# PV in two runs of four units: one PSUM tile for two batches, and new instruction orders, in a graph and attention kernel

## The chip, the cores and the metric

One Trainium2 chip, one core. The metric is the device time of one execution in microseconds (us), from the profiler's first to last event of the core. The kernel before takes 847.73 us, the median of three runs (845.4 to 847.89).

## What is computed

x is (128, 128, 256) in float32: 128 independent batches of 128 nodes with 256 features. Two residual layers follow each other, and both see the same 128x128 adjacency.

```
h = relu(layernorm(x))
x = x + L0(h)      # a per-row number: max over features of (adj h) and a bias, relu
h = relu(layernorm(x))
q, k, v = h @ w_qkv                     # 8 heads of 32
attn = softmax(mask(q k^T / sqrt(32)))  # masked where adj == 0
o = (attn @ v) @ w_proj + b_proj
x = x + o + layernorm(o) * gamma + beta
```

Because L0 gives one number per row, the second layer norm of x needs no new statistics; the kernel adds that number at the end. To keep float32 accuracy with fp16 matmuls, most operands are split into a high and a low fp16 part, and three products of parts are summed.

## The kernel before

**Tiling.** The batches go in 32 groups of G = 4. A group passes through four steps of a software pipeline, so step t works on group t (layer 0, q, k and v), group t-1 (scores and their row maxima), group t-2 (transposed scores, exponentials, PV and row sums) and group t-3 (1/row sum, output projection, layer norm, store). There are 35 steps (`pipeline`, L215).

**Five programs, each with a written order.** Each engine runs the same list of items in every step; the list is the string ORDER of that engine. Each item is a letter and a number, and semaphores tie them together. A change of an ORDER string moves work in that engine's queue and nothing else.

TensorE (L278 to L477):
- K0, K1 (`mask_scores`, L333) and N0, N1 (`mask_scores_T`, L364) put the mask into the four PSUM tiles sc_ps by 16 matmuls of 32x32 tiles each. S0 to S7 (`scores`, L344) and E0 to E7 (`scores_T`, L372) add q k^T and k q^T, four matmuls each; a unit of S is a batch and half the heads. K1 waits for the exponentials of E3, N1 for the row maxima of S7.
- S0 and S4 wait until the stacks of q and k parts have landed (`stacked`). M0 (`transpose_max`, L356) transposes the row maxima; it waits until all four o tiles are read, since they share a PSUM bank.
- Q0 to Q3 (`project_qk`, L296), V0, V1 (`project_v`, L313) and L0, L1 (`layer0`, L287) share two PSUM tiles a_ps. Q0 and Q2 use the first, Q1 and Q3 the second, and V0 and V1 likewise; V0 waits for both parts of Q2, V1 for those of Q3.
- P0 to P7 (`values`, L384) multiply the exponentials of a unit (one batch, four heads) by v, in four column tiles of 32 (L400), and add the row sums in the same way (L403): 16 matmuls of 128 columns in float32 counted as two passes. P0 waits for the parts of the row maxima (`clo_ready`), since sum_ps is one bank. The PSUM tile pv_ps has room for four units, but `values` writes only its first two: P2, P4 and P6 wait until ScalarE has copied the batch before (`pv_ready`).
- R0 to R3 (`spread`, L407) spread the reciprocal row sums of a batch over the partitions, into pv_ps; O0 to O3 (`project_o`, L419) project o, into o_ps, one batch at a time.

ScalarE (L480 to L615): E0 to E7 are the exponentials (`exps`, L550), each into one of P_SLOTS = 4 buffers, so that E4 waits for P0, and so on to E7 for P3. Q0 to Q3 (`qk_high`) copy the high part of q or k; A0 to A3 (`take_pv`, L556) copy PV of a batch; C0 to C3 (`o_high`, L562), O0 to O3 (`take_o`), R and H (rectify x and its high part), M0 (`max_high`, L545), V0, V1 (`take_v`). T0 (`transpose_h`, L509) issues the DMA that transposes h from ScalarE's queue, when the low parts H0 to H3 of GpSimd are done; X0 (L528) issues the load of x three groups ahead.

VectorE (L620 to L743): S0 to S7 are the row maxima (`row_max`, L650), Q0 to Q3 the low parts of q and k (`qk_low`, L643), O0 to O3 scale o (`scale_o`, L678), I0 to I2 invert the row sums, M0 is the low part of the row maxima, L0 and L1 the maxima of layer 0, X0 and X1 the statistics of x, B and G those of o, F0 to F3 the last elementwise work (`finish`, L697), two instructions each; F0 and F1 belong to batches 0 and 1.

GpSimd (L791 to L872): C0 to C3 low parts of o (`o_low`, L818), H0 to H3 low parts of h, N0 and W0 to W3 the layer norm's factors, D0 the accumulating store of y, X0 the factors of x.

SyncE's DMA queue (L225 to L275): Q0 and Q1 (`stack_heads`, L248) each issue 12 DMAs that stack the parts of q and k by heads, when the low parts of Q1, or of Q3, are there; M0 (L241) issues two for the row maxima; C0 (`copy_x`, L235) copies x into the output, which the store adds to.

Of the kernel before, what the change touches and what calls it, by code (L numbers as in the profile page):

```python
# [56 lines left out]
def build(nc, x, adj, bias0, w_qkv, w_proj, b_proj, gamma, beta, out):  # L57
# [3 lines left out]
    with ExitStack() as ctx:  # L61
# [559 lines left out]
        def _(dve):  # L621
# [56 lines left out]
            def scale_o(g, b):  # L678
                dve.wait_ge(r_psum, G * g + b + 1)
                dve.wait_ge(pv_ready, G * g + b + 1)  # L680
                if b == 0:
                    wait(dve, ohi_ready, G * g)
# [243 lines left out]
```

## Time and profile before

| | |
|---|---|
| median of the runs | 847.73 us |
| the profiled execution | 843.2 us |
| its span, first to last instruction | 841.3 us |
| TensorE busy | 752.9 us, 89% |
| VectorE busy | 612.7 us, 73% |
| ScalarE busy | 496.4 us, 59% |
| GpSimd busy | 394.3 us, 47% |
| DMA engines, mean of 16 | 66% over three queues |
| TensorE clock granted, mean | 0.973 |

The profiled execution itself took 843.2 us, 4.5 us less than the median of the runs. Times of instructions are microseconds from the start of the span. A matmul row shows when the first of its matmuls began and how long until the last ended; ends overlap the next group's start. "PEld" are weight loads, "ACTq" and "SPq" the queues that issue DMAs. The step that is used for most rows is step 19; it begins with K0 at 471.20.

### The profile page before, as it was taken

The page shows a single profiled execution, that of the slowest core. Times are in us where ns is not written, and L with a number is a line of the kernel's source. Part 1 is how long each engine was busy: PE and PEld are TensorE (multiplying, and loading weights), DVE is VectorE, ACT ScalarE, POOL GpSimd, SP SyncE. Part 2 cuts the span into 40 slices and gives each one's busy share as a digit, 9 for nine tenths or more (in the row PEclk, how much of TensorE's full clock was granted, in tenths as well). Part 3 has the DMA queues.
Part 4 walks back from the last instruction along what each step waited for, and adds up shares of the span by engine and source line. Part 5 has one row for each costly group of instructions (what it writes and reads, how often), then busy time and mean ns, then how long its engine had stood idle before and what let it go on. Part 6 is the DMA issues. An engine that isn't in the chain of part 4 may idle for free.

```text
span 841.3 us, 28575 instructions
## 1 busy us (share of the span) xinstructions
PE 752.9 (89%) x11113; PEld 502.6 (60%) x11113; DVE 612.7 (73%) x1488; ACT 496.4 (59%) x1160; POOL 394.3 (47%) x724
## 2 busy tenths in 40 slices
PE   0668999999999999999999999999999999999662
PEld 0235666666666666666666666666666666666441
DVE  4744677777788877777788777787778887777642
ACT  3234666656666666666666666666666766655440
POOL 5712254554554444444554444554455454443442
PEclk9888999999999999999999999999999999999985
DMA  6355577778876767867767777777786887674321
GB/s 196 75 154 138 134 151 160 150 144 165 165 164 157 165 137 149 158 157 163 175 158 154 166 148 171 143 155 165 167 172 154 165 159 148 127 135 105 58 37 25
DMA packets 167285, 121.36 MB, mean 144 GB/s; under 512 B 83696, under 2 KB 166384, under 8 KB 166640
## 3 DMA queue, kind: packets, MB, share of 16 engines
q1 hardware_dynamic: 67328, 69.72, 31.2%
q10 hardware_dynamic: 82928, 33.04, 21.0%
q0 software_dynamic: 16896, 16.78, 14.3%
q8 instruction: 89, 1.46, 0.7%
q14 instruction: 44, 0.36, 0.1%
HBM read 35.06 MB, written 33.55 MB: 82 GB/s over the span
## 4 chain that ended last, share of the span: by engine, by line
PE 58%; DVE 13%; SPq 10%; issue 9%; DMA 4%; POOL 3%; ACT 3%; ACTq 1%; DVEq 0%; POOLq 0%
PE a_ps L307 13%; SPq L261 10%; DVE smax L655 9%; PE a_ps L320 7%; PE pv_ps L400 7%; PE sc_ps L380 6%; PE sum_ps L403 5%; PE sc_ps L329 5%; PE sum_ps L430 4%; PE sc_ps L352 4%; DMA stack<-pairs 3%; PE a_ps L292 2%; PE pv_ps L415 1%; POOL stack L894 1%; DVE st L688 1%
## 5 line engine op out<-in xcount | busy, mean ns | idle before, releaser
L655 DVE TENSOR_REDUCE smax<-sc_ps 128x4 f32<-128x512 f32 x256 | 164.4, 684 | 26.6 <-PE sc_ps L352 24.7
L647 DVE TENSOR_TENSOR pairs<-a_ps,pairs 128x512 f16<-128x512 f32 x128 | 87.3, 683 | 118.6 <-ACT pairs L543 118.5
L553 ACT ACTIVATE p_sb<-sc_ps 128x512 f32<-128x512 f32 x256 | 146.3, 602 | 41.0 <-PE sum_ps L403 34.3
L816 POOL TENSOR_TENSOR h_parts<-h_sb,h_parts 128x256 f16<-128x256 f32 x128 | 84.3, 670 | 137.0 <-ACT h_parts L507 136.7
L307 PE MATMUL a_ps<-hT,w_hi 128*128 128x512 f16 x512 | 135.6, 388 | 13.8 <-DMA hT<-h_parts 13.8
L822 POOL TENSOR_TENSOR oT_lo<-oT,oT_hi 128x256 f16<-128x256 f32 x128 | 85.6, 669 | 105.6 <-ACT oT_hi L566 105.3
L543 ACT ACTIVATE pairs<-a_ps 128x512 f16<-128x512 f32 x128 | 76.2, 596 | 98.1 <-issue 59.1
L400 PE MATMUL pv_ps<-p_sb,v_sb 128*32 128x128 f32 x2048 | 107.4, 278 | 16.4 <-ACT pv_sb L560 9.8
L850 POOL DMA_DIRECT2D out<-y_sb x32 | 43.1, 1348 | 162.3 <-DVE y_sb L710 162.3
L403 PE MATMUL sum_ps<-p_sb,sel_sum 128*32 128x128 f32 x2048 | 105.7, 273 | 0.0
L352 PE MATMUL sc_ps<-stack 96*128 96x128 f16 x1024 | 84.3, 222 | 11.0 <-DMA stack<-pairs 10.9
L352 PEld LDWEIGHTS sc_ps<-stack 96*128 96x128 f16 x1024 | 65.3, 99 | 34.3 <-DMA stack<-pairs 14.7
L400 PEld LDWEIGHTS pv_ps<-p_sb,v_sb 128*32 128x32 f32 x2048 | 52.3, 109 | 55.1 <-issue 47.7
L566 ACT ACTIVATE oT_hi<-oT 128x256 f16<-128x256 f32 x128 | 53.0, 414 | 48.4 <-DVE oT L684 48.3
L380 PE MATMUL sc_ps<-stack 98*128 98x128 f16 x1024 | 80.0, 222 | 0.0
L320 PE MATMUL a_ps<-w_hi,hT 128*128 128x256 f16 x512 | 77.2, 273 | 1.9 <-DVE pairs L647 1.9
L307 PEld LDWEIGHTS a_ps<-hT,w_hi 128*128 128x128 f16 x512 | 43.1, 99 | 59.7 <-issue 25.1
L307 PE MATMUL a_ps<-hT,w_lo 128*128 128x512 f16 x256 | 77.5, 385 | 0.0
L499 ACT ACTIVATE h_sb<-x_sb,shift,rstd 128x256 f32<-128x256 f32 x128 | 72.0, 588 | 7.3 <-POOL shift L809 7.3
L572 ACT ACTIVATE o_sb<-sum_ps 128x256 f32<-128x256 f32 x128 | 48.6, 380 | 44.8 <-PE sum_ps L430 42.0
L380 PEld LDWEIGHTS sc_ps<-stack 98*128 98x128 f16 x1024 | 63.8, 99 | 15.1 <-issue 13.8
L684 DVE TENSOR_TENSOR oT<-pv_ps,pv_sb 128x256 f32<-128x256 f32 x128 | 53.2, 416 | 24.0 <-PE pv_ps L415 24.0
(94 smaller groups left out, 1415.3 us busy)
## 6 DMA issues: line engine op xcount, KB each, us to landing
stack<-pairs SPq DMA_DIRECT2D x768, 64.0 KB, 3.0
out<-in_x SPq DMA_DIRECT2D x32, 512.0 KB, 4.0
out<-y_sb POOLq DMA_DIRECT2D x32, 512.0 KB, 6.6
x_sb<-in_x ACTq DMA_DIRECT2D x31, 512.0 KB, 6.0
stack<-crow SPq DMA_DIRECT2D x64, 8.0 KB, 4.1
w_sb<-in_L_gnn_w_qkv SPq DMA_DIRECT2D x1, 768.0 KB, 5.4
x_sb<-in_x SPq DMA_DIRECT2D x1, 512.0 KB, 4.3
hT<-h_parts ACTq DMA_TRANSPOSE x32, 5.9
```

What stands on the lines that cost most here:

```text
L261: nc.sync.dma_start(dst.rearrange("p s b n -> p s (b n)"), src).then_inc(stacked[j], 16)
L307: mm = nc.tensor.matmul(a_ps[c % 2][:].rearrange("p (b n) -> p b n", b=G), w[:, dc, col:col + P], hT[:, par, part, :, dc], start=(k == 0), ...
L320: mm = nc.tensor.matmul(a_ps[i][:, bb * D:(bb + 1) * D], hT[:, par, part, 2 * i + bb, dc], w[:, dc, 2 * D:3 * D], start=(k == 0), stop=(k ...
L352: mm = nc.tensor.matmul(to[:, i], stack[0:STACK, par, 0, h, b], stack[0:STACK, par, 1, h, b], start=False, stop=True, skip_group_check=True)
L380: mm = nc.tensor.matmul(to[:, i], stack[0:ROWS, par, 1, h, b], stack[0:ROWS, par, 0, h, b], start=False, stop=True, skip_group_check=True)
L400: nc.tensor.matmul(pv_ps[HD * i:HD * (i + 1), j], v_sb[:, par, b, HD * h:HD * (h + 1)], p_sb[:, u % P_SLOTS, i], start=True, stop=True)
L403: mm = nc.tensor.matmul(sum_ps[HD * i:HD * (i + 1), 0], sel_sum[:, u], p_sb[:, u % P_SLOTS, i], start=(u == 0), stop=(u == UNITS - 1), ski ...
L553: nc.scalar.activation(p_sb[:, u % P_SLOTS], sc_ps[u % SC_SLOTS][:], ACT.Exp, scale=SCALE).then_inc(p_ready, 1)
L647: nc.vector.tensor_tensor(pairs[:, 1 - c % 2, c // 2, c % 2], a_ps[c % 2][:], pairs[:, c % 2, c // 2, c % 2], ALU.subtract).then_inc(qklo_ ...
L655: nc.vector.tensor_reduce(smax[:, HC * j:HC * (j + 1), b], sc_ps[u % SC_SLOTS][:], AX.X, ALU.max).then_inc(smax_ready, 1)
L816: nc.gpsimd.tensor_tensor(h_parts[:, par, 1, b], h_sb[:, b], h_parts[:, par, 0, b], ALU.subtract).then_inc(hlo_ready, 1)
L822: nc.gpsimd.tensor_tensor(oT_lo[:, b], oT[:, b], oT_hi[:, b], ALU.subtract).then_inc(olo_ready, 1)
```

## The change

- `pv_ps` is now used in full: PV of unit u goes to slot u % 4 (PAIR = 2 * DC = 4), so the tile holds two batches. `values` waits for `pv_ready` and `v_ready` at units 0 and 4 alone.
- `take_pv`, `spread`, `scale_o` and `o_high` go by two batches: two of each in a step, each twice as wide (128x512, and four matmuls in `spread`). `o_low`, `project_o` and `take_o` stay by one batch. The semaphores count pairs accordingly.
- The ORDER strings of all five programs are new. On TensorE the eight P units stand in two runs of four, where there were four runs of two.

```
-PE   "K0 S0 S1 R0 S2 Q0 S3 R1 Q1 N0 E0 R2 O0 E1 E2 E3 L0 O1 R3 K1 S4 S5 O2 S6 S7 L1 O3 N1 M0 E4 E5 E6 "
-     "P0 P1 Q2 P2 P3 Q3 P4 P5 E7 V0 P6 P7 V1"
+PE   "K0 S0 S1 S2 R0 Q0 S3 Q1 N0 E0 R1 E1 O0 E2 E3 L0 O1 K1 S4 S5 S6 O2 L1 S7 O3 N1 E4 E5 E6 M0 E7 Q2 "
+     "P0 P1 P2 P3 Q3 V0 P4 P5 P6 P7 V1"
-ACT  "C0 Q0 R0 R1 C1 Q1 E0 C2 O0 E1 E2 E3 H0 O1 X0 C3 R2 O2 H1 H2 O3 R3 M0 H3 E4 A0 T0 Q2 A1 E5 Q3 E6 "
-     "E7 A2 V0 A3 V1 L0"
+ACT  "R0 R1 C0 Q0 H0 Q1 E0 E1 C1 O0 E2 E3 O1 X0 R2 O2 H1 R3 H2 O3 H3 M0 T0 E4 Q2 E5 L0 E6 E7 A0 Q3 V0 "
+     "A1 V1"
-DVE  "I0 I1 I2 S0 O0 S1 S2 S3 O1 Q0 O2 X0 Q1 L0 B0 O3 S4 B1 S5 S6 S7 B2 B3 M0 X1 G0 L1 Q2 F0 Q3 F1 F2 F3"
+DVE  "I0 I1 I2 S0 S1 O0 S2 S3 O1 Q0 Q1 X0 B0 S4 B1 S5 S6 S7 L0 B2 B3 M0 G0 L1 Q2 F0 F1 X1 F2 Q3 F3"
-POOL "C0 C1 C2 H0 C3 H1 H2 H3 N0 W0 W1 W2 W3 K0 D0 X0"
+POOL "C0 C1 H0 C2 C3 H1 H2 H3 N0 W0 W1 W2 W3 K0 D0 X0"
-SP   "C0 Q0 M0 Q1"
+SP   "Q0 M0 Q1 C0"
```

```diff
             def values(g, par, u, sc):
                 b, j = u // DC, u % DC
                 pe.wait_ge(p_ready, UNITS * g + u + 1)
-                if j == 0:
-                    if b % 2 == 0:
-                        pe.wait_ge(v_ready, 2 * g + b // 2 + 1)
-                    wait(pe, pv_ready, G * g + b)
+                if u % PAIR == 0:
+                    pe.wait_ge(v_ready, 2 * g + b // 2 + 1)
+                    wait(pe, pv_ready, 2 * g + b // 2)
...
-                    nc.tensor.matmul(pv_ps[HD * i:HD * (i + 1), j], v_sb[:, par, b, HD * h:HD * (h + 1)],
+                    nc.tensor.matmul(pv_ps[HD * i:HD * (i + 1), u % PAIR], v_sb[:, par, b, HD * h:HD * (h + 1)],
...
-            def spread(g, b):
+            def spread(g, i):
...
-                for j in range(DC):
-                    mm = nc.tensor.matmul(pv_ps[:, j], sel_row[:, b * DC + j].rearrange("p h d -> p (h d)"), rpair[:],
+                for n in range(PAIR):
+                    mm = nc.tensor.matmul(pv_ps[:, n], sel_row[:, PAIR * i + n].rearrange("p h d -> p (h d)"), rpair[:],
...
-            def take_pv(g, b):
-                act.wait_ge(pv_psum, UNITS * g + DC * (b + 1))
+            def take_pv(g, i):
+                act.wait_ge(pv_psum, UNITS * g + PAIR * (i + 1))
...
-                nc.scalar.activation(pv_sb[:, b], pv_ps[:, 0:DC], ACT.Copy).then_inc(pv_ready, 1)
+                nc.scalar.activation(pv_sb[:, 2 * i:2 * i + 2].rearrange("p b c n -> p (b c) n"), pv_ps[:],
+                                     ACT.Copy).then_inc(pv_ready, 1)
...
-                nc.scalar.activation(oT_hi[:, b], oT[:, b], ACT.Copy).then_inc(ohi_ready, 1)
+                nc.scalar.activation(oT_hi[:, 2 * i:2 * i + 2], oT[:, 2 * i:2 * i + 2], ACT.Copy).then_inc(ohi_ready, 1)
...
-                nc.vector.tensor_tensor(oT[:, b], pv_ps[:, 0:DC], pv_sb[:, b], ALU.mult).then_inc(oT_ready, 1)
+                nc.vector.tensor_tensor(oT[:, 2 * i:2 * i + 2].rearrange("p b c n -> p (b c) n"), pv_ps[:],
+                                        pv_sb[:, 2 * i:2 * i + 2].rearrange("p b c n -> p (b c) n"),
+                                        ALU.mult).then_inc(oT_ready, 1)
```

## Rows read from the trace of the kernel before

**Rows 1.** The page, part 4: the chain that ended last, by engine.

```profile
PE 58%; DVE 13%; SPq 10%; issue 9%; DMA 4%; POOL 3%; ACT 3%; ACTq 1%; DVEq 0%; POOLq 0%
```

**Rows 2.** Timeline of TensorE: K0 of step 4 and of step 31. Start, length, instruction.

```profile
114.89 0.43 PE L329 MATMUL sc_ps<-mask_q,identb 32*32 32x512 bf16 x16
...
752.22 0.43 PE L329 MATMUL sc_ps<-mask_q,identb 32*32 32x512 bf16 x16
```

**Rows 3.** Timeline of TensorE, step 19: K0, S0, K1's S4, N1, M0.

```profile
471.20 0.43 PE L329 MATMUL sc_ps<-mask_q,identb 32*32 32x512 bf16 x16
471.57 0.62 PE L352 MATMUL sc_ps<-stack 96*128 96x128 f16 x8
...
479.52 0.62 PE L352 MATMUL sc_ps<-stack 96*128 96x128 f16 x8
...
482.82 0.44 PE L329 MATMUL sc_ps<-mask_k,identb 32*32 32x512 bf16 x16
483.34 0.27 PE L361 MATMUL sum_ps<-identf,smax 128*32 128x128 f32 x1
483.45 0.83 PE L380 MATMUL sc_ps<-stack 98*128 98x128 f16 x12
```

**Rows 4.** Timeline of TensorE, step 19: P0, P1, Q2, P2, Q3, P4 (first rows of each).

```profile
484.47 0.42 PE L400 MATMUL pv_ps<-p_sb,v_sb 128*32 128x128 f32 x8 [0.19 <-DVE crow L661]
...
484.91 0.43 PE L400 MATMUL pv_ps<-p_sb,v_sb 128*32 128x128 f32 x8
...
485.49 1.04 PE L307 MATMUL a_ps<-hT,w_hi 128*128 128x512 f16 x4
...
486.89 0.43 PE L400 MATMUL pv_ps<-p_sb,v_sb 128*32 128x128 f32 x8
...
487.90 1.04 PE L307 MATMUL a_ps<-hT,w_hi 128*128 128x512 f16 x4
...
489.32 0.43 PE L400 MATMUL pv_ps<-p_sb,v_sb 128*32 128x128 f32 x8
```

**Rows 5.** Timeline of ScalarE, step 19: X0, M0, T0, Q2. The bracket is idle time before.

```profile
479.21 0.38 ACTq L532 DMA_DIRECT2D x_sb<-in_x  x1
...
483.64 0.27 ACT L548 ACTIVATE crow<-sum_ps 32x128 f16<-32x128 f32 x1
...
485.69 2.51 ACTq L514 DMA_TRANSPOSE hT<-h_parts  x1
...
488.31 0.60 ACT L543 ACTIVATE pairs<-a_ps 128x512 f16<-128x512 f32 x1 [2.20 <-issue]
```

**Rows 6.** Timeline of VectorE, step 19: X1, Q2, F0, Q3.

```profile
484.15 0.36 DVE L634 BATCH_NORM_AGGREGATE mv<-st 128x2 f32<-128x6 f32 x4
...
488.93 0.69 DVE L647 TENSOR_TENSOR pairs<-a_ps,pairs 128x512 f16<-128x512 f32 x1 [3.59 <-ACT pairs L543]
489.54 0.87 DVE L704 SCALAR_TENSOR_TENSOR t_sb<-o_sb,mv,w_sb 128x256 f32<-128x256 f32 x2
490.33 0.68 DVE L647 TENSOR_TENSOR pairs<-a_ps,pairs 128x512 f16<-128x512 f32 x1
```

**Rows 7.** Timeline of SyncE's DMA queue: stacks of Q3 in steps 15 and 19.

```profile
397.63 9.24 SPq L261 DMA_DIRECT2D stack<-pairs  x12
...
491.09 9.96 SPq L261 DMA_DIRECT2D stack<-pairs  x12
```

**Rows 8.** Timeline of the weight loads: S4 of step 16.

```profile
409.47 0.45 PEld L352 LDWEIGHTS sc_ps<-stack 96*128 96x128 f16 x8 [0.41 <-DMA stack<-pairs]
```

**Rows 9.** The view of line L514, T0: all 32 issues.

```profile
L514 ACTq DMA_TRANSPOSE hT<-h_parts x32: 1431/2511/3746, 15.5 to 743.5; - x32
```

**Rows 10.** The view of line L261, the stacks: from one DMA's issue to its landing.

```profile
DMA to landing us min/median/max: 2.0/3.0/6.4
```

**Rows 11.** Groups by line with their shapes: busy, mean ns of one, idle before.

```profile
L684 DVE TENSOR_TENSOR oT<-pv_ps,pv_sb 128x256 f32<-128x256 f32 x128 | 53.2, 416 | 24.0 <-PE pv_ps L415 24.0
```

**Rows 12.** The page, part 6: DMA issues with size and time to landing.

```profile
x_sb<-in_x ACTq DMA_DIRECT2D x31, 512.0 KB, 6.0
```

More of the change, by code:

```diff
@@ L50 @@
 P_SLOTS = 4
+PAIR = 2 * DC
 PAIRS = 4 * DC * G * N
@@ L387, in values @@
                 pe.wait_ge(p_ready, UNITS * g + u + 1)
-                if j == 0:
-                    if b % 2 == 0:
-                        pe.wait_ge(v_ready, 2 * g + b // 2 + 1)
-                    wait(pe, pv_ready, G * g + b)
+                if u % PAIR == 0:
+                    pe.wait_ge(v_ready, 2 * g + b // 2 + 1)
+                    wait(pe, pv_ready, 2 * g + b // 2)
                 if u == 0:
-                    wait(pe, oT_ready, G * g)
+                    wait(pe, oT_ready, 2 * g)
                     wait(pe, rsum_ready, g)
@@ L554, in exps, with o_high @@
                                      scale=SCALE).then_inc(p_ready, 1)
-            def take_pv(g, b):
-                act.wait_ge(pv_psum, UNITS * g + DC * (b + 1))
-                if b == 0:
-                    wait(act, oT_ready, G * g)
-                nc.scalar.activation(pv_sb[:, b], pv_ps[:, 0:DC], ACT.Copy).then_inc(pv_ready, 1)
-            def o_high(g, b):
-                act.wait_ge(oT_ready, G * g + b + 1)
-                if b == 0:
+            def take_pv(g, i):
+                act.wait_ge(pv_psum, UNITS * g + PAIR * (i + 1))
+                if i == 0:
+                    wait(act, oT_ready, 2 * g)
+                nc.scalar.activation(pv_sb[:, 2 * i:2 * i + 2].rearrange("p b c n -> p (b c) n"), pv_ps[:],
+                                     ACT.Copy).then_inc(pv_ready, 1)
+            def o_high(g, i):
+                act.wait_ge(oT_ready, 2 * g + i + 1)
+                if i == 0:
                     wait(act, o_psum, G * g)
-                nc.scalar.activation(oT_hi[:, b], oT[:, b], ACT.Copy).then_inc(ohi_ready, 1)
+                nc.scalar.activation(oT_hi[:, 2 * i:2 * i + 2], oT[:, 2 * i:2 * i + 2], ACT.Copy).then_inc(ohi_ready, 1)
             def take_o(g, b):
@@ L673, in invert_sums, with scale_o @@
                     dve.wait_ge(rsum16_ready, g + 1)
-                    wait(dve, r_psum, G * g)
+                    wait(dve, r_psum, 2 * g)
                     nc.vector.scalar_tensor_tensor(rpair[:], rsum16[:], lo_rows[:, 0:1], rsum[:], ALU.mult,
                                                    ALU.add).then_inc(rpair_ready, 1)
[L678 to L682, printed above, removed]
+            def scale_o(g, i):
+                dve.wait_ge(r_psum, 2 * g + i + 1)
+                dve.wait_ge(pv_ready, 2 * g + i + 1)
+                if i == 0:
+                    wait(dve, ohi_ready, 2 * g)
                     wait(dve, olo_ready, G * g)
-                nc.vector.tensor_tensor(oT[:, b], pv_ps[:, 0:DC], pv_sb[:, b], ALU.mult).then_inc(oT_ready, 1)
+                nc.vector.tensor_tensor(oT[:, 2 * i:2 * i + 2].rearrange("p b c n -> p (b c) n"), pv_ps[:],
+                                        pv_sb[:, 2 * i:2 * i + 2].rearrange("p b c n -> p (b c) n"),
+                                        ALU.mult).then_inc(oT_ready, 1)
             def stats_o(g, b):
```

27 lines of the change are left out of this document (13 added, 14 removed).

## The prediction

> **What bounds the kernel now.** I read the chain of waits first: TensorE holds 58% of it, and SyncE's DMA queue with its transfers another 14% [rows 1]. So there are two candidates, TensorE's own order and some loop that runs through SyncE. The period tells which holds when. K0 of step 4 starts at 114.89 and K0 of step 31 at 752.22 [rows 2]: 637.33 us in 27 steps, a mean of 23.60. Step 19, where TensorE hardly waits, lasts 23.20 (471.20, and K0 of step 20 at 494.40 by the same view). The mean lies 0.4 above what TensorE's order needs.
>
> The second bound is a ring that closes once per step, and the timelines of four engines give it piece by piece. S4 on TensorE at 479.52 needs the stack of q and k; from it come the row maxima, N1 at 482.82 and M0 at 483.34 [rows 3]; ScalarE reads M0 at 483.64, issues the transpose T0 at 485.69 for 2.51 us, and only then takes Q2, at 488.31: the bracket says it sat idle 2.20 us for "issue", with Q2 of TensorE long finished [rows 5]. VectorE follows with Q2 at 488.93 and Q3 at 490.33 [rows 6], SyncE starts its 12 stack DMAs at 491.09 [rows 7], and S4 of the next step waits for the last of them. From S4 to the first stack DMA it is 491.09 - 479.52 = 11.57. From the first DMA to a released S4: in step 15 it began at 397.63 [rows 7] and S4 of step 16, which did wait for it, at 409.47 [rows 8], 11.84. Between the bounds: twelve issues take 9.24 to 9.96 [rows 7]; less the last one's 0.64 and with a landing of 2.0 to 3.0 [rows 10] that is 10.6 to 12.3. I take the middle, 11.45. The ring of now is 11.57 + 11.45 = 23.02, just under the 23.20 of TensorE's order. Whenever T0 is longer than 2.51 (it reaches 3.7 [rows 9]) or the landing is late, the ring wins; that is where the 0.4 comes from.
>
> **Part 1, TensorE's order.** Nothing is added or removed among the matmuls; PV, row sums, `spread` and projections have the same counts. What goes:
> - Two of four runs of P. A run costs on both sides. Six matmuls of Q2 at 0.216 (1.04 less a length of 0.39, over three) are 1.30, but P2 comes 1.40 after Q2: 0.10 to enter. P1 to Q2 is 0.58 where P0 to P1 is 0.44 [rows 4]: 0.15 to leave. Two runs: 2 x 0.25 = 0.49.
> - P0's wait for the row maxima. E4 to E6 end 12 x 0.056 = 0.67 after 483.45 [rows 3], and 0.10 for entry gives 484.22; P0 starts at 484.47 [rows 4]. 0.25, hidden in future by E7 and Q2 (0.22 + 1.30), which stand between M0 and P0. If that cover went, 0.25 would return.
> - M0's wait for the last o tile. N1 to M0 is 0.52, K0 to S0 0.37 [rows 3]: 0.15, hidden by E4 to E6.
> - The wait of P2, P4 and P6 for the copy of one batch becomes one of P4 for two. In step 19 it is nothing (487.90 to 489.32 is 1.42, the same as 1.40) [rows 4]. In the new order Q3 and V0 stand before P4, but ScalarE has E4, Q2, E5, L0, E6, E7 before its copy. I reckon 0 to 0.2.
>
> The order then needs 23.20 - 0.49 - 0.25 - 0.15 = 22.3, to 22.5 with that wait. Alone it would be worth 23.6 - 22.5 = 1.1 us a step.
>
> The trace shows that entering and leaving column tiles costs TensorE 0.10 and 0.15 us [rows 4]. The Trainium skill (TensorEngine Tiling (Array Packing), Tiling Modes) says that a change of tiling mode drains TensorE; the trace agrees. By that rule alone the change would win some 0.5 a step, 14 us.
>
> **Part 2, VectorE, ScalarE, GpSimd.** `scale_o` takes 416 ns for 256 columns [rows 11] and, from the nearest row of 512, 0.69 [rows 6]: two for four saves 0.3 a step on an engine 73% busy, and nothing on TensorE's path: R1 now waits for a tile of 0.69 in place of 0.42, but stands behind Q0, S3, Q1, N0 and E0. The copies of 512 columns cost 0.60 [rows 5]. All that is off both paths; cost 0, between -0.3 and +0.3.
>
> **Part 3, the ring, new.** I count from S4, with durations of step 19.
> 1. S4 to N1: the same three S units, O2, L1 and O3 stand between, and the same four row maxima and one statistics instruction on VectorE: 3.30 [rows 3].
> 2. N1 to M0: 0.37 + three E units of 0.22 = 1.04, for 0.52 before. M0 at 4.34.
> 3. ScalarE's M0 at +0.30 [rows 3, 5], and T0, now directly behind it and in front of E4, some 0.27 later (M0's own length; GpSimd's low part of H3 ends about then): 4.91. T0 holds the queue 2.51, and the next starts 0.11 after [rows 5]: E4 at 7.53, Q2 behind it at 8.03 (0.60 long, the overlap of back-to-back work takes about 0.1).
> 4. VectorE's Q2 0.62 later: 8.65; the next starts 0.61 after [rows 5, 6]: 9.26. Here the new order puts F0, F1, X1 and F2 before Q3, where there was F0 alone. A pair F costs 0.79 (489.54 to 490.33), X1 about 0.30 (0.36 long) [rows 6]: 3 x 0.79 + 0.30 = 2.67. Q3 at 11.93.
> 5. SyncE starts 0.76 after (490.33 to 491.09) [rows 6, 7]: 12.69.
> 6. The landing: 11.45. C0, the copy of x, has moved from before Q0 to after Q1, the same place in the cycle, so the queue has the same two neighbours. What waits behind SyncE's stack DMAs is C0 and then Q0 of the next step, which is not late.
>
> Sum 24.14 for 23.02 before: +1.1. T0 comes earlier in the ring (4.91 for 6.17, 485.69 - 479.52), which saves 1.26; E4 behind it gives 0.50 back, and Q3 behind F1, X1 and F2 costs 1.88. The rest, 0.0, closes it: 11.57 - 1.26 + 0.50 + 1.88 = 12.69. Q2 also lets V0 go late by 0.1 to 0.2 on TensorE, which is off the ring.
>
> So the ring, not TensorE, sets the period: 24.14. There is no slack of 0.2 to swallow a long T0 any more, so every variation of T0 and of the landing passes through: I take 24.2. Against 23.60 it is +0.60 over the 28 steps in which the ring is closed, +16.8; at the end, where nothing is stacked, the shorter order gives about 0.8 back. Sum +16: the profiled execution of 843.2 becomes 859. It stands 4.5 below the median of the runs, 847.73; on the median's scale I forecast **863.5 us**, 1.9% slower.
>
> **Rivals.**
> A, TensorE is the bound (faster). If the ring came below 22.5, the period would be 22.5: 28 x -1.1 = -31, 817 us. It needs a landing of 9.8 or less. For it: twelve unhindered issues of 0.64 and 2.0 make 9.0. Against: neither row of 12 issues is near 7.7 [rows 7]. Chance 0.12.
> B, the ring binds but is shorter by 0.5 to 1.2, since T0 issues in 2.0 or stacks land in 10.6, both inside their rows [rows 9, 10]: period 23.0 to 23.7, 831 to 850 us. It decides against me from a ring of 23.6, so 0.54 off my sum. Chance 0.20, of which 0.08 lies within 0.3% of no change (about what a measurement of this kernel can tell from none).
> C, the landing gets longer (slower still). X0, the load of x, is issued at 479.21, 0.31 before S4 [rows 5, 3]. It hangs on O1, not on S4; with S4 late it starts about 1.4 before S4, beside the last stacks, and needs 6.0 to land [rows 12]. If the last 1.4 ran at half rate, +0.7 and 36 us in all: 874 to 884 us. Chance 0.16.
> The Trainium skill (DMA: Bandwidth & Descriptors, Queues, rings and completion order) says that each DMA engine goes round the queue rows by packets, so a second queue takes its share; no row here isolates it, and its case is C's.
> D, the change does not do what it says: P4 waits for its copy as long as P2, P4 and P6 did. Worth 0.2 a step, 6 us, inside my forecast's range.
>
> **How the numbers follow.** Forecast (ring 23.8 to 24.6, 852 to 874 us) 0.52; A 0.12; B 0.20; C 0.16. Faster 0.12 + 0.12 = 0.24, same 0.08, slower 0.52 + 0.16 = 0.68. The range 836 to 880 leaves out A and part of B (0.13) and the top of C (0.06). The forecast's own range is 852 to 874.
>
> **What the new profile would show.** P runs of four units with one entry and exit each; M0 and P0 without idle time before them; K1 to S4 with about 1.4 us of idle time, released by the stack DMAs, in nearly every step; "issue" before E4 rather than before Q2 on ScalarE; SyncE's second dozen starting 12.7 after S4. I am wrong if S4 waits in few steps, if the dozen starts under 12.1 after S4, or if its landing is under 11. A gain with S4 not waiting would be A.

## The result, and the profile after the change

| | before | after |
|---|---|---|
| median of 5 runs | 847.73 us (845.4 to 848.78) | 868.32 us (866.44 to 869.51) |
| ratio, with its 95% interval | | 1.0259 (1.0224 to 1.0294) |
| profiled execution: time, span | 843.2, 841.3 us | 866.44, 864.5 us |
| mean period, K0 of step 4 to K0 of step 31 | 23.60 us | 24.33 us |

The changed kernel is 2.6% slower. The forecast was 863.5 us, and the measured median lies 4.8 us above it. Two of the ten executions of the kernel with X0 late (below) were slow, one with 965.59 us at a granted clock of 0.748, and its ratio leaves both out though its median counts them.

**What bounds it.** The first part of the page of the changed kernel gives the engines' busy time; the chain that ended last, by engine, is its fourth part.

```profile
PE 749.8 (87%) x11113; PEld 504.0 (58%) x11113; DVE 603.9 (70%) x1424; ACT 469.1 (54%) x1032; POOL 395.2 (46%) x724
...
SPq 29%; DVE 22%; PE 19%; DMA 8%; issue 7%; ACTq 6%; ACT 4%; POOL 3%; DVEq 0%; POOLq 0%
```

TensorE held 58% of the chain before [rows 1] and holds 19% now; SyncE's queue with its transfers went from 14% to 37%, VectorE from 13% to 22%, ScalarE's queue from 1% to 6%. That is the ring: S4, row maxima, N1, M0, T0, Q2, the pairs F, Q3, twelve stack DMAs ("the dozen"), their landing, S4. No engine does more work: VectorE and ScalarE have 64 and 128 instructions fewer than before and less busy time in all.

The waits of TensorE between 100 and 740 us, changed kernel: line, releaser, us in total, times, longest.

```profile
PE sc_ps L353 <- DMA stack<-pairs: 16.0, 21, 2.5
PE a_ps L321 <- DVE pairs L648: 14.0, 20, 1.1
PE sum_ps L427 <- ACT o_sb L573: 5.0, 22, 0.3
```

And the same view of the kernel before:

```profile
PE pv_ps L400 <- DVE crow L661: 5.5, 27, 0.3
PE pv_ps L400 <- ACT pv_sb L560: 5.2, 10, 0.8
PE sc_ps L352 <- DMA stack<-pairs: 3.0, 5, 1.2
```

P's two small waits are gone, as the change was made to do, 10.7 us in all. In their place stand S4's for the stack, V0's for Q2 (L321) and O1's for its accumulator (L427), 35.0 us.

**One turn of the ring, step 12.** TensorE's timeline of the changed kernel, from S4 of step 12 (the scores right behind K1) to K0 of step 13, with S4 of step 13 as the last row:

```profile
325.18 0.84 PE L353 MATMUL sc_ps<-stack 96*128 96x128 f16 x12 [0.27 <-DMA stack<-pairs]
...
328.49 0.44 PE L330 MATMUL sc_ps<-mask_k,identb 32*32 32x512 bf16 x16
...
329.54 0.27 PE L362 MATMUL sum_ps<-identf,smax 128*32 128x128 f32 x1
...
331.27 0.43 PE L400 MATMUL pv_ps<-p_sb,v_sb 128*32 128x128 f32 x8
...
333.15 1.04 PE L308 MATMUL a_ps<-hT,w_hi 128*128 128x512 f16 x4
...
335.17 0.60 PE L321 MATMUL a_ps<-w_hi,hT 128*128 128x256 f16 x4 [0.55 <-DVE pairs L648]
...
336.58 0.43 PE L400 MATMUL pv_ps<-p_sb,v_sb 128*32 128x128 f32 x8
...
339.88 0.43 PE L330 MATMUL sc_ps<-mask_q,identb 32*32 32x512 bf16 x16
...
349.81 0.45 PE L353 MATMUL sc_ps<-stack 96*128 96x128 f16 x5 [0.92 <-DMA stack<-pairs]
```

ScalarE's: M0, T0, E4, Q2.

```profile
329.85 0.27 ACT L548 ACTIVATE crow<-sum_ps 32x128 f16<-32x128 f32 x1 [0.69 <-PE sum_ps L362]
330.01 3.11 ACTq L514 DMA_TRANSPOSE hT<-h_parts  x1
333.22 0.60 ACT L553 ACTIVATE p_sb<-sc_ps 128x512 f32<-128x512 f32 x1 [3.10 <-PE sum_ps L403]
333.71 0.59 ACT L543 ACTIVATE pairs<-a_ps 128x512 f16<-128x512 f32 x1
```

VectorE's: Q2, then F0 and F1 (two L707, two L713), X1 (L635), F2, and only then Q3.

```profile
334.34 0.69 DVE L648 TENSOR_TENSOR pairs<-a_ps,pairs 128x512 f16<-128x512 f32 x1 [3.05 <-ACT pairs L543]
334.94 0.87 DVE L707 SCALAR_TENSOR_TENSOR t_sb<-o_sb,mv,w_sb 128x256 f32<-128x256 f32 x2
335.73 0.87 DVE L713 SCALAR_TENSOR_TENSOR y_sb<-t_sb,base,beta_sb 128x256 f32<-128x256 f32 x2
336.52 0.37 DVE L635 BATCH_NORM_AGGREGATE mv<-st 128x2 f32<-128x6 f32 x4
336.82 0.84 DVE L707 SCALAR_TENSOR_TENSOR t_sb<-o_sb,mv,w_sb 128x256 f32<-128x256 f32 x2
337.58 0.68 DVE L648 TENSOR_TENSOR pairs<-a_ps,pairs 128x512 f16<-128x512 f32 x1
```

SyncE's queue, the dozen of Q3:

```profile
338.34 9.98 SPq L262 DMA_DIRECT2D stack<-pairs  x12
```

The four lists read as one chain: 325.18 to N1 at 328.49 is 3.31, to M0 1.05, to T0 0.47, T0 itself 3.11 and 0.10 to E4, 0.49 to Q2, 0.63 to VectorE's Q2, 3.24 to Q3, 0.76 to the first stack DMA, together 13.16; from there to the next S4 11.47. One turn is 24.63 us. ScalarE's bracket before E4 blames a PE line that had ended long before: P's row sums of the step before. What stood in front of E4 was T0, issued from the same queue and 3.11 long; a bracket whose releaser had long finished does not name what held the instruction.

TensorE's list shows what the change gained: one run of P from 331.27 and one from 336.58, each entered and left once, and neither M0 nor P0 has a bracket. It also shows V0 at 335.17, 2.02 after Q3 began, where six matmuls and their hand-over would take 1.30.

**Over steps 6 to 27**, worked out from the trace in this way. The rows that do not say median are means.

| us | forecast | after |
|---|---|---|
| S4 to N1; to M0; to T0, medians | 3.30; 4.34; 4.91 | 3.30; 4.35; 4.83 |
| the same, means | | 3.44; 4.49; 4.97 |
| T0, median of all issues | 2.51 | 3.02 (mean 2.86) |
| VectorE, Q2 to Q3 | 3.28 | 3.30 (median 3.24) |
| S4 to the first DMA of the dozen | 12.69 | 13.17 (12.19 to 13.87) |
| first DMA to the last landing | 11.45 | 11.12 (10.55 to 12.97) |
| landing to S4 | 0, always | 0.05, in every step |
| period | 24.2 | 24.33 |

In the kernel before, the same means are 11.74 to the dozen, 11.39 for the landing and then 0.51 in which the stack lay ready and TensorE came late. Now 13.17 + 11.12 + 0.05 = 24.34: S4 waits for the landing in every step, so the ring is the period.

**TensorE's clock.** Medians and means of the first row differ because of two steps, 7 and 21. In them S4 had waited 2.5 and 2.4 us for the stack, with TensorE idle, and the granted clock then stood at 0.50 (1.2 in place of 2.4 GHz) for 3.4 us. Here is the view of windows for step 7 (the granted clock is the third value from the right), with S4 and N1 of that step:

```profile
197.80:204.50 6.70, 4.27 (x69) 2.80 (x53) 3.52 (x8) 4.99 (x12) 3.23 (x5) 1.00 0.76 190
204.60:207.90 3.30, 3.15 (x20) 2.47 (x21) 2.21 (x4) 0.15 (x1) 0.00 (x0) 0.50 0.91 259
```

```profile
204.75 1.46 PE L353 MATMUL sc_ps<-stack 96*128 96x128 f16 x12 [2.46 <-DMA stack<-pairs]
...
209.56 0.44 PE L330 MATMUL sc_ps<-mask_k,identb 32*32 32x512 bf16 x16
```

The twelve matmuls of S4 take 1.46 where they take 0.84 in step 12, and N1 starts 4.81 after S4 in place of 3.30 (4.74 in step 21). The kernel before has the clock at 1.00 all the way from step 4 to step 31. In the twelve traces of this document there are 324 steps between K0 of step 4 and K0 of step 31. Of these, 19 hold a stretch at 0.50, and they last 25.95 us or more; none of the other 305 lasts over 25.73. In all 19, S4 had waited 1.8 to 4.7 us for the stack just before. A late ring thus costs more than its own wait. That the wait brings the clock down was not tested by itself, and not every wait does (`before_x_early`, step 12: 2.19 us, and the clock stays at 1.00).

### The profile page after: what moved, and what is told of

The parts are those of the page before. It is cut to its first block, busy times and chain, and to the rows that moved or that the text cites. A ratio compares the mean times of both kernels' runs of the same rounds, so it can differ in the third digit from the quotient of the medians.

```text
span 864.5 us, 28255 instructions
## 1 busy us (share of the span) xinstructions
PE 749.8 (87%) x11113; PEld 504.0 (58%) x11113; DVE 603.9 (70%) x1424; ACT 469.1 (54%) x1032; POOL 395.2 (46%) x724
## 3 DMA queue, kind: packets, MB, share of 16 engines
q0 software_dynamic: 16896, 16.78, 14.5%
q8 instruction: 89, 1.46, 0.7%
## 4 chain that ended last, share of the span: by engine, by line
SPq 29%; DVE 22%; PE 19%; DMA 8%; issue 7%; ACTq 6%; ACT 4%; POOL 3%; DVEq 0%; POOLq 0%
SPq L262 29%; DVE smax L656 8%; DMA stack<-pairs 8%; DVE t_sb L707 6%; ACTq L514 6%; PE a_ps L308 4%; PE sc_ps L381 4%; DVE y_sb L713 2%; PE sc_ps L353 2%; DVE pairs L648 2%; ACT pairs L543 2%; PE sc_ps L330 2%; PE pv_ps L400 2%; PE sum_ps L430 2%; PE sum_ps L403 1%
## 5 line engine op out<-in xcount | busy, mean ns | idle before, releaser
L553 ACT ACTIVATE p_sb<-sc_ps 128x512 f32<-128x512 f32 x256 | 142.7, 606 | 92.1 <-PE sum_ps L403 90.4
L648 DVE TENSOR_TENSOR pairs<-a_ps,pairs 128x512 f16<-128x512 f32 x128 | 85.1, 683 | 97.6 <-ACT pairs L543 97.5
L824 POOL TENSOR_TENSOR oT_lo<-oT,oT_hi 128x256 f16<-128x256 f32 x128 | 83.1, 670 | 89.9 <-ACT oT_hi L567 89.8
L400 PE MATMUL pv_ps<-p_sb,v_sb 128*32 128x128 f32 x2048 | 105.1, 276 | 3.7 <-ACT pv_sb L560 3.0
L353 PE MATMUL sc_ps<-stack 96*128 96x128 f16 x1024 | 81.4, 224 | 26.7 <-DMA stack<-pairs 26.2
L403 PE MATMUL sum_ps<-p_sb,sel_sum 128*32 128x128 f32 x2048 | 103.6, 273 | 0.0
L321 PE MATMUL a_ps<-w_hi,hT 128*128 128x256 f16 x512 | 77.1, 273 | 15.6 <-DVE pairs L648 15.6
L381 PE MATMUL sc_ps<-stack 98*128 98x128 f16 x1024 | 83.4, 222 | 0.0
L381 PEld LDWEIGHTS sc_ps<-stack 98*128 98x128 f16 x1024 | 65.0, 99 | 16.2 <-issue 14.9
L685 DVE TENSOR_TENSOR oT<-pv_ps,pv_sb 128x512 f32<-128x512 f32 x64 | 43.9, 686 | 40.4 <-PE pv_ps L415 40.4
L400 PEld LDWEIGHTS pv_ps<-p_sb,v_sb 128*32 128x32 f32 x2048 | 56.9, 109 | 23.8 <-issue 20.2
L321 PEld LDWEIGHTS a_ps<-w_hi,hT 128*128 128x128 f16 x512 | 45.9, 97 | 39.0 <-ACT pairs L543 23.8
```

Source lines behind the costliest of these rows:

```text
L321: mm = nc.tensor.matmul(a_ps[i][:, bb * D:(bb + 1) * D], hT[:, par, part, 2 * i + bb, dc], w[:, dc, 2 * D:3 * D], start=(k == 0), stop=(k ...
L353: mm = nc.tensor.matmul(to[:, i], stack[0:STACK, par, 0, h, b], stack[0:STACK, par, 1, h, b], start=False, stop=True, skip_group_check=True)
L381: mm = nc.tensor.matmul(to[:, i], stack[0:ROWS, par, 1, h, b], stack[0:ROWS, par, 0, h, b], start=False, stop=True, skip_group_check=True)
L400: nc.tensor.matmul(pv_ps[HD * i:HD * (i + 1), u % PAIR], v_sb[:, par, b, HD * h:HD * (h + 1)], p_sb[:, u % P_SLOTS, i], start=True, stop=True)
L403: mm = nc.tensor.matmul(sum_ps[HD * i:HD * (i + 1), 0], sel_sum[:, u], p_sb[:, u % P_SLOTS, i], start=(u == 0), stop=(u == UNITS - 1), ski ...
L553: nc.scalar.activation(p_sb[:, u % P_SLOTS], sc_ps[u % SC_SLOTS][:], ACT.Exp, scale=SCALE).then_inc(p_ready, 1)
```

## The experiments

All kernels were timed against the kernel before on the same chip; a ratio is the kernel's time over that of the kernel before (843.05 to 846.39 us there). My theory is the ring; its rival is that the wider tiles or TensorE's new order cost the time by themselves. None of the expectations has a term for TensorE's clock.

### Landing shortened, in both kernels

The store of y, which adds into `out` from GpSimd's queue, is cut to 16 of its 128 rows; nothing on an engine's path changes.

```diff
-                nc.gpsimd.dma_start(og[g], y_sb[:], accum_op=ALU.add).then_inc(stored, 16)
+                nc.gpsimd.dma_start(og[g][0:16], y_sb[0:16], accum_op=ALU.add).then_inc(stored, 16)
```

> The changed kernel, but the store of y covers only 16 of the 128 rows of each batch; the rest of the output lacks the last addition. The question is whether the ring (S4, M0, T0, Q2, Q3, the dozen stack DMAs, their landing, S4) sets the period. Ring theory: the store shares the DMA engines with the dozen, so without most of it the dozen lands in about 10.0 us in place of 11.1 (mean, from its first issue), and the whole 1.1 a step comes off: 868 - 30 = about 838 us. Rival, the loss lies on TensorE's side (the wider copies, V0 and P4 waiting) and the stacks only seem late: the landing gets shorter and the period stays within 0.3 of 24.3, 860 us or more.

> The kernel before with the same store of 16 rows in 128; the rest of the output lacks the last addition. Ring theory: here TensorE's own order needs 23.2 of the 23.6 us of a step, so however early the dozen lands, no more than about 0.3 a step comes off: 838 to 843 us, a gain of 5 to 10 us against some 30 in the changed kernel with the same edit. Rival (the store slows every kernel alike, through memory or the engines): both kernels gain the same.

Changed kernel: 836.51 us, ratio 0.9889 (0.9826 to 0.9952), against 1.0259 with the whole store. Kernel before: 835.5 us, ratio 0.9895 (0.986 to 0.9931). The same edit is worth 3.6% in one and 1.05% in the other. The landing fell by 1.3 us in both (11.12 to 9.84, 11.39 to 10.14), the period from 24.33 to 23.38 and from 23.60 to 23.38. TensorE's waits in the changed kernel with the small store, 100 to 740 us:

```profile
PE a_ps L321 <- DVE pairs L648: 17.2, 22, 1.3
PE sc_ps L353 <- DMA stack<-pairs: 1.3, 4, 0.4
```

S4's 16.0 us are 1.3, and the clock stays at 1.00 from step 4 to step 31. V0's wait stays, so it belongs to another loop. That a transfer which no engine waits for makes the difference between the two kernels speaks for the ring and against a cost of tiles or matmuls.

### One segment of the ring lengthened in the kernel before

Q3 on VectorE put behind F1 and F2, as the change has it; nothing else.

```diff
-  "... M0 X1 G0 L1 Q2 F0 Q3 F1 F2 F3"
+  "... M0 X1 G0 L1 Q2 F0 F1 F2 Q3 F3"
```

> The kernel before with one move in VectorE's order: Q3 behind F1 and F2, as the change has it (tiles, TensorE, ScalarE as before). Ring theory: first stack DMA 1.6 us later after S4 (13.3 for 11.7), ring 13.3 + 11.4 = 24.7, +1.1 a step, some 30 us: about 875. Rival, Q3's place costs nothing since SyncE waits for something else or V1 hides it: under 852.

890.1 us, ratio 1.0567 (1.05 to 1.0635): this one move of the change, alone, costs twice what the whole change costs. From S4 to the dozen it is 13.40 instead of 11.74 on the mean, and TensorE's first wait between 100 and 740 us is now:

```profile
PE sc_ps L352 <- DMA stack<-pairs: 35.6, 21, 4.7
```

It is 15 us slower than I expected, and four steps lasted 29.1 to 30.6 us. Each has two things in it. The first is a landing of 14.5 to 14.9 just before, on which S4 waits over 4 us. The second is the clock: it then stands at 0.50 for 3.4 us, once for 6.8, and S4 to N1 takes 4.8 and once 6.1 in place of 3.3. With a fifth such step, of 26.7 us, the clock costs 8.9 us between S4 and N1 alone. The long landings bring the mean landing to 11.87, 12.7 us in 27 steps. The two together are more than what I missed by; in the steps at full clock S4 to the dozen is 13.10, under my 13.3.

X0, the load of x, began some 5 us before S4 in the four, but that is because S4 came late: it starts 9.8 to 10.0 after the dozen's first DMA there, and 9.7 to 10.9 after it in the steps that land in 10.4 to 12.6 too. What goes with the four long landings is a slow issue, 10.8 to 11.2 for the dozen where it is 9.0 to 10.5 in the others. In the kernel before, where X0 stands 11.4 after the first DMA, two dozens of 10.9 landed in 12.4; so a slow issue that reaches into the load of x may be what makes them 14.5 and more. No run here separates the two.

### The load of x beside the stacks (rival C)

In the kernel before, X0 moves to the head of ScalarE's order.

```diff
-  "C0 Q0 R0 R1 C1 Q1 E0 C2 O0 E1 E2 E3 H0 O1 X0 C3 ..."
+  "X0 C0 Q0 R0 R1 C1 Q1 E0 C2 O0 E1 E2 E3 H0 O1 C3 ..."
```

> The kernel before with only X0 moved, to the head of ScalarE's order. The load of x then starts about 3.4 us after the dozen. Contention theory: the dozen takes 13.1 us for 11.4, the ring 11.7 + 13.1 + 0.05 = 24.9 closes over TensorE's 23.2, and the time rises by 1.2 a step, some 33 us, to about 877. Rival, two transfers side by side just share idle bandwidth (the DMA engines are 76% busy): landing within 0.4 of before, under 855 us.

876.56 us, ratio 1.0407 (1.0378 to 1.0435), as expected. SyncE's queue, then ScalarE's, then the weight load of the S4 that follows:

```profile
335.66 9.36 SPq L261 DMA_DIRECT2D stack<-pairs  x12
...
339.49 0.38 ACTq L532 DMA_DIRECT2D x_sb<-in_x  x1
...
348.69 0.45 PEld L352 LDWEIGHTS sc_ps<-stack 96*128 96x128 f16 x8 [1.36 <-DMA stack<-pairs]
```

The dozen is issued in the usual time, 9.36 us, yet S4 starts 13.03 after its first DMA. On the mean the landing went from 11.39 to 13.36: 512 KB whose transfer lies wholly beside the dozen add 2.0 us, and the load itself takes 8.0 us by its median where it took 6.0 [rows 12]. The Trainium skill (DMA: Bandwidth & Descriptors, Queues, rings and completion order) says that a DMA engine goes round the queue rows packet by packet; that both transfers are longer together agrees with it. In the changed kernel X0 stands 0.90 before S4 on the mean, and 10.3 after the dozen's first DMA in nearly every step. Its landing is 11.12 all the same, so rival C added nothing to the mean. The two landings of 12.90 and 12.97 stand before the two steps at half clock; why they are long is open. In the kernel with X0 at the head the clock falls to 0.50 in four of the 27 steps, each time behind a wait of S4.

### Parts of the ring shortened in the changed kernel

Q2 directly behind T0 on ScalarE, for E4 first:

```diff
-  "... M0 T0 E4 Q2 E5 L0 E6 E7 A0 Q3 V0 A1 V1"
+  "... M0 T0 Q2 E4 E5 L0 E6 E7 A0 Q3 V0 A1 V1"
```

> The changed kernel with one swap in ScalarE's order: Q2 directly behind T0, E4 behind Q2. It takes one exponential, 0.48 us, out of the ring and touches nothing else. Ring theory: 0.4 a step less, 868 - 11 = about 857 us, and first stack DMA of Q3 about 12.7 after S4 in place of 13.2. Rival, VectorE is late for Q3 anyway since it works off F0 to F2: no gain, since F0 starts when Q2 is done, this rival could only hold if VectorE were busy before Q2, where the trace shows it idle. Second rival: E4 to E7 get late and P4 waits for its copy, 0.3 or more a step, no gain.

A miss: 871.63 us, ratio 1.0327 (1.0284 to 1.0369), not the 857 I expected. From S4 to the dozen it fell to 12.92 only, and the landing rose by 0.6 to 11.76. TensorE's waits:

```profile
PE sc_ps L353 <- DMA stack<-pairs: 26.4, 22, 4.1
PE pv_ps L400 <- ACT pv_sb L560: 6.7, 16, 0.6
PE a_ps L321 <- DVE pairs L648: 6.3, 12, 1.1
```

V0's wait halved, P4 waits for its copy (rival D), and the longest S4 wait is 4.1 for 2.5. The clock falls three times, once for 6.8 us, where it fell twice before. With the steps touched by that left out, S4 to the dozen is 12.70 for 13.09 in the changed kernel, so the swap did give the 0.4 that I expected of it; but the landing is 11.61 for 11.08 in the same steps, which takes it back. Why the landing grew is not settled by this run.

Q3 early on both engines of its way:

```diff
 ScalarE
-  "... M0 T0 E4 Q2 E5 L0 E6 E7 A0 Q3 V0 A1 V1"
+  "... M0 T0 E4 Q2 E5 Q3 L0 E6 E7 A0 V0 A1 V1"
 VectorE
-  "... L1 Q2 F0 F1 X1 F2 Q3 F3"
+  "... L1 Q2 F0 Q3 F1 X1 F2 F3"
```

> The changed kernel with Q3 alone moved: on ScalarE behind E5, on VectorE behind F0 (so F1, X1 and F2 come after it). It undoes the part of the change that I price highest. Ring theory: the first stack DMA comes at most 11.4 after S4 in place of 13.2, the stacks no longer hold S4 in most steps, and the period falls to the next bound, T0 in front of Q2 and so of V0, about 23.8: 868 - 14 = about 854 us. Rival, T0's issue alone is to blame: no gain over 3 us.

855.25 us, ratio 1.0125 (1.0054 to 1.0196), as expected, against 1.0259. The dozen starts 11.28 after S4 instead of 13.17. TensorE's waits:

```profile
PE pv_ps L400 <- ACT pv_sb L560: 18.3, 27, 1.1
PE a_ps L321 <- DVE pairs L648: 11.6, 18, 1.0
PE sc_ps L353 <- DMA stack<-pairs: 1.4, 2, 0.8
```

The ring is open and S4 no longer waits, but the gain is 13 us, not the 1.89 a step that the ring gave: ScalarE now reaches the copy A0 later, so P4 waits 0.7 a step, and V0 still waits for Q2 behind T0. Three conditions hang on one engine's order, and undoing one brings up the next.

### New orders on three engines, X0 first and X0 late

TensorE's order stays that of the change; ScalarE, VectorE and GpSimd get new ones. The two kernels differ only in X0's place.

```diff
 ScalarE
-  "R0 R1 C0 Q0 H0 Q1 E0 E1 C1 O0 E2 E3 O1 X0 R2 O2 H1 R3 H2 O3 H3 M0 T0 E4 Q2 E5 L0 E6 E7 A0 Q3 V0 A1 V1"
+  "X0 R0 H0 C0 Q0 R1 H1 Q1 E0 E1 O0 E2 E3 C1 O1 R2 H2 O2 R3 H3 O3 M0 T0 Q2 E4 E5 Q3 A0 E6 E7 A1 V0 L0 V1"
   (second kernel: X0 between O2 and R3)
 VectorE
-  "I0 I1 I2 S0 S1 O0 S2 S3 O1 Q0 Q1 X0 B0 S4 B1 S5 S6 S7 L0 B2 B3 M0 G0 L1 Q2 F0 F1 X1 F2 Q3 F3"
+  "I0 I1 I2 S0 O0 S1 S2 S3 Q0 X0 Q1 X1 O1 L0 B0 S4 S5 S6 S7 B1 B2 B3 G0 M0 L1 F0 Q2 F1 Q3 F2 F3"
 GpSimd
-  "C0 C1 H0 C2 C3 H1 H2 H3 N0 W0 W1 W2 W3 K0 D0 X0"
+  "C0 H0 C1 H1 C2 C3 H2 H3 N0 K0 W0 W1 X0 W2 W3 D0"
```

> The changed kernel with TensorE's order, tiles and wide copies untouched, and new orders for ScalarE, VectorE and GpSimd: statistics B2, B3 and G0 before M0, F0 before Q2 and only F1 between Q2 and Q3 on VectorE; on ScalarE Q2 directly behind T0 and Q3 before E6; H1 to H3 earlier. By the durations of the trace the ring falls from 24.3 to 22.5 and TensorE's order, 22.4 to 22.6, becomes the bound. Ring theory: period 22.6, 868 - 1.7 x 28 = about 821 us, below the 848 of the kernel before; the gain of the runs of four shows once the ring is out of the way. Rival, the tile for two batches costs on TensorE or ScalarE by itself: not under 848.

> The run after_three_orders was 854 us where 821 had been expected: its ring up to the first stack DMA did fall to 11.1 us, but the dozen took about 12.9 us to land in place of 11.1, and there ScalarE's order had put the load of x (X0) at the head of the step, 3.4 us after the dozen's start. This kernel is the same but for X0, which stands behind O2, so after S4, when no dozen is in flight. Contention theory: the landing returns to 11.1 to 11.4, the period falls from 24.0 to 22.6 to 22.9, about 854 - 34 = 820 us. Rival, the shorter ring makes the landing long in some other way (SyncE's queue fuller, the store): the landing stays over 12.4 and the time over 840.

With X0 first: 854.48 us, ratio 1.0117 (1.0068 to 1.0166). With X0 late: 836.01 us, ratio 0.9894 (0.9858 to 0.993). Both missed my 821 and 820, and by different things. X0 first, SyncE's dozen, the load of x and the next S4:

```profile
328.48 9.30 SPq L262 DMA_DIRECT2D stack<-pairs  x12
...
331.79 0.38 ACTq L532 DMA_DIRECT2D x_sb<-in_x  x1
...
341.21 0.45 PEld L353 LDWEIGHTS sc_ps<-stack 96*128 96x128 f16 x8 [1.50 <-DMA stack<-pairs]
```

X0 late, the same three:

```profile
324.00 9.49 SPq L262 DMA_DIRECT2D stack<-pairs  x12
...
335.62 0.67 PEld L353 LDWEIGHTS sc_ps<-stack 96*128 96x128 f16 x12 [0.23 <-issue]
...
337.34 0.38 ACTq L532 DMA_DIRECT2D x_sb<-in_x  x1
```

In the first, x comes 3.3 after the dozen's first DMA and S4 starts 12.73 after it; in the second, x comes after S4 and S4 starts 11.62 after. The mean landings are 12.9 and 11.70, the periods 24.03 and 23.31. From S4 to the dozen it is 11.1 and 11.3, some 1.9 less than in the changed kernel; X0's place alone is worth the other 2.2%, with what the clock adds: it fell three times in the first and once in the second. The second stays 1.0 above the 22.3 that TensorE's order needs. That goes with a ring of 11.32 + 11.70 = 23.0 and a wait of V0 of 0.46 a step.

### New orders on four engines, with the changed tiles and with those of before

First the changed tiles:

```diff
 TensorE
-  "... R0 Q0 S3 Q1 N0 E0 R1 E1 O0 E2 E3 L0 O1 K1 S4 S5 S6 O2 L1 S7 O3 N1 E4 E5 E6 M0 E7 Q2 P0 P1 P2 P3 Q3 V0 ..."
+  "... R0 Q0 S3 Q1 N0 E0 R1 E1 O0 E2 E3 L0 O1 K1 S4 S5 O2 S6 S7 L1 O3 N1 E4 M0 E5 E6 Q2 E7 Q3 P0 P1 P2 P3 V0 ..."
 ScalarE
+  "R0 Q0 H0 C0 Q1 E0 E1 C1 O0 E2 E3 R1 O1 R2 H1 X0 O2 H2 R3 H3 O3 M0 T0 Q2 Q3 E4 E5 A0 L0 E6 E7 A1 V0 V1"
 VectorE
+  "I0 I1 I2 S0 S1 O0 S2 S3 Q0 O1 Q1 B0 B1 S4 S5 S6 S7 B2 L0 B3 G0 M0 L1 X0 X1 Q2 Q3 F0 F1 F2 F3"
 GpSimd
+  "H0 C0 C1 C2 C3 H1 H2 H3 N0 K0 W0 W1 W2 W3 X0 D0"
```

> The changed tiles with new orders for TensorE, ScalarE, VectorE and GpSimd: M0 behind E4, Q2 and Q3 before P0, Q2 and Q3 directly behind T0 on ScalarE and behind each other on VectorE, X0 between H1 and O2. By the durations of the traces the ring is 9.6 + 11.2 = 20.8 and TensorE's order needs 22.2: period 22.2 to 22.5, about 868 - 1.9 x 28 = 814 us, well below the kernel before. If the landing grows over 12.5, or T0 makes Q0 of the next step late, it would be 22.8 or more, over 825 us.

808.16 us, ratio 0.9588 (0.9557 to 0.9619). It beats the kernel before by 4.1% and the changed one by 6.5% (0.9588 / 1.0259). Its chain:

```profile
PE 74%; SPq 6%; ACTq 5%; DVE 4%; POOL 3%; DMA 3%; issue 2%; ACT 2%; DVEq 0%; POOLq 0%
```

All waits of TensorE that the view lists between 100 and 700 us:

```profile
PE a_ps L321 <- DVE pairs L648: 3.4, 7, 0.8
PE sc_ps L353 <- DMA stack<-pairs: 0.9, 3, 0.4
```

K0 of step 4 and of step 31:

```profile
111.88 0.43 PE L330 MATMUL sc_ps<-mask_q,identb 32*32 32x512 bf16 x16
...
716.95 0.43 PE L330 MATMUL sc_ps<-mask_q,identb 32*32 32x512 bf16 x16
```

605.07 / 27 = 22.41, and eleven of the 27 steps last 22.20 to 22.21, which is what the order of matmuls needs. From S4 to the dozen it is 9.74: M0 stands behind one E unit instead of three, and Q2 and Q3 go through ScalarE and VectorE before anything that can wait. With a landing of 11.79 the ring takes 21.53, and 0.84 of slack stands before S4. This is rival A, at an order of 22.2 where I had 22.3 to 22.5.

Then new orders of the same aim for the kernel before, its tiles and its copies by one batch kept:

```diff
 TensorE
-  "K0 S0 S1 R0 S2 Q0 S3 R1 Q1 N0 E0 R2 O0 E1 E2 E3 L0 O1 R3 ... Q3 P4 P5 E7 V0 P6 P7 V1"
+  "K0 S0 S1 S2 R0 Q0 S3 R1 Q1 R2 N0 E0 O0 E1 E2 L0 E3 O1 R3 ... Q3 E7 P4 P5 V0 P6 P7 V1"
 ScalarE
+  "R0 C0 H0 R1 Q0 C1 Q1 H1 E0 C2 O0 E1 E2 E3 O1 C3 R2 X0 O2 H2 R3 O3 M0 H3 E4 A0 T0 Q2 A1 E5 Q3 E6 A2 E7 V0 A3 L0 V1"
 VectorE
+  "I0 I1 I2 S0 O0 S1 S2 S3 O1 O2 Q0 X0 Q1 B0 O3 B1 S4 S5 S6 S7 X1 L0 B2 B3 M0 G0 L1 F0 Q2 Q3 F1 F2 F3"
 GpSimd
+  "H0 C0 C1 C2 H1 C3 H2 H3 N0 W0 W1 X0 W2 W3 D0 K0"
```

> The tiles, copies and four runs of two P units of the kernel before, with new orders for TensorE, ScalarE, VectorE and GpSimd worked out in the same way as those of all_orders (808 us): Q3 behind Q2 and F0 before them on VectorE, X0 of ScalarE behind S4. It asks whether orders alone give that gain. Tile theory: four runs of two keep two entries and exits (0.5), the waits of P2, P4 and P6 and P0's wait, so TensorE needs 23.0 to 23.4: about 836 to 842 us, at most 1% faster than before. Rival, the gain of all_orders was in the other engines' orders and the tile adds nothing: under 820 us.

845.28 us, ratio 1.0001 (0.9969 to 1.0033): nothing, and above the 836 to 842 that I expected. TensorE's order still needs 23.18, and the period is 23.51, with one step of 26.71 at half clock in it. Only this one set of orders was tried, so it does not show that none would help; but TensorE's order, not the ring, bounds this one, where with the changed tiles it bounds at 22.20. The difference, 23.18 - 22.20 = 0.98 a step, is what the two runs of P and the waits that go with them are worth, provided that the ring stays under TensorE's order. It is an estimate, since the two kernels also place M0, E5 to E7, Q2 and Q3 differently on TensorE.

## Why the prediction was right

**The sign, the mechanism and nearly the size were right.** A shorter landing, an earlier Q3 and new orders on all engines each take nearly all of S4's wait away, and each time the loss over the kernel before shrinks or turns round (1.0259 to 0.9889, 1.0125, 0.9588); lengthening the Q3 segment alone in the kernel before makes S4's wait and a loss of 5.7%. The rival that the tiles cost time by themselves falls with the fastest kernel, which has them. What the prediction lacked is a term for TensorE's clock, and most of the distance between 863.5 and 868.3 lies there ("From step to span").

By the steps of the prediction:

- **Part 1, TensorE's order.** M0 and P0 wait for nothing, and P4 does not wait for its copy. The period of 24.33 less S4's mean idle time of 0.67, V0's 0.65, O1's 0.35 and some 0.2 in small pieces (E1 to O0, E3 to L0, and 0.1 for the steps at half clock) is 22.5, in the 22.3 to 22.5 forecast; the kernel with all orders shows 22.20 without a wait.
- **Part 2, the wide operations.** The estimate for `scale_o` was 0.69 us, and the row by line and shape of the changed kernel has 686 ns:

```profile
L685 DVE TENSOR_TENSOR oT<-pv_ps,pv_sb 128x512 f32<-128x512 f32 x64 | 43.9, 686 | 40.4 <-PE pv_ps L415 40.4
```

  43.9 us for 53.2 before [rows 11], 0.29 a step, off the path as said.
- **Part 3, steps 1 and 2.** 3.30 and 4.35, for 3.30 and 4.34, in all steps at full clock.
- **Step 3 is the term that was mis-sized.** T0 was put at 2.51, its median before [rows 9]. In the new place it takes 3.02 by its median:

```profile
L514 ACTq DMA_TRANSPOSE hT<-h_parts x32: 1405/3024/3655, 14.3 to 767.0; - x32
```

  By its mean of steps 6 to 27, 2.86, T0 is 0.35 over my 2.51 (short ones of 1.4 pull the mean under the median); in the kernel before that mean is 2.58, so 0.07 of it came from taking a median. From S4 to the dozen I had 12.69, and it was 13.17 on the mean. Of these 0.48, T0 has 0.35, and 0.14 are the two steps at half clock, spread over 22. In the other 20 steps it is 13.1.
- **Steps 4 and 5.** 3.30 on the mean (3.24 in step 12) for 3.28, and 0.76 for 0.76.
- **Step 6, the landing.** 11.12 for 11.45. It is 0.33 shorter than forecast and makes up for nearly all of T0, so the period came out at 24.33 for 24.2 though two of its terms were off. That these two cancel is luck. The 0.06 that the forecast put on for variation was not worked out from rows.
- **V0** was to go late by 0.1 to 0.2 and goes late by 0.65, since T0, earlier in front of Q2, holds Q2 on ScalarE and VectorE. It cost nothing on the ring, as said, but it is why K1 to S4 shows 0.67 of idle time and not 1.4: part of the wait is spent at V0 and O1 instead.
- **From step to span.** 27 steps cost 19.65 (656.98 - 637.33), in place of 16.2. Of this the two stretches at half clock have 2.95 between S4 and N1 (1.51 and 1.44); without them it is 16.7. The end gave back 0.7, as forecast (0.8). I had counted one of the first three steps with 0.6; those three took 73.41 for 69.48, 3.9 more, and the start another 0.4. There, too, the clock differs: before K0 of step 4 it stands at 0.50 for 20.5 us in the kernel before and for 30.7 in the changed one. At the 1.51 us that a stretch of 3.41 cost in step 7, 10.2 us more are some 4.5, an estimate, and the start is 4.3 longer. So the ring was forecast well, and what was left out at no price is the clock. The profiled execution is thus 23.2 slower, against a forecast of 16. The median of the runs is only 20.6 slower, because the profiled execution of before stood 4.5 below its median and that of after 1.9.
- **Rivals.** A needed a ring under 22.5 and is what the all-orders kernel does. B did not come: T0 got longer, not shorter. C did not show: the mean landing is 11.12, under my 11.45, and the two long steps are those at half clock. D is nothing here (Q3 and V0 cover it) and shows at 0.7 a step once Q3 is put early.
- **What the new profile would show.** S4 waits in every step, the dozen starts over 12.1 after it and the landing is over 11, as said. The bracket before E4 does not say "issue" but names P's row sums.

## What to carry to other kernels

Where four queues pass one item round per step, add up the ring item by item, with the issuing time of every DMA in it, and set it beside the bounding engine's own order before making that engine shorter: here they stood 0.2 us apart, and a change that took a microsecond off TensorE and put a microsecond on the ring lost 2.6%. Look at the granted clock of the longest steps before explaining them by anything else: a sum over a mean step has no term for it. The reorder pays when the ring's own items go first on each engine they cross (Q2 and Q3 before E and F), and transfers that nothing waits for are kept away from the ring's transfers. A wait that vanishes in the view of waits is no gain by itself: read which line waits in its stead.
